# A decoder block on one core: score groups of both kinds in one slot, the router's negated maximum on ScalarE, and later slots for what shares its bank

## The reference

```
x = layernorm(x + mixer(x))            # y = (s + D) * gated, y @ W_out.T + b_out + x
q, k, v = x @ Wq.T + bq, ctx @ Wk.T + bk, ctx @ Wv.T + bv      # 16 heads of 16
x = layernorm(x + softmax(q k^T / 4) v @ Wo.T + bo)
idx, pmax = argmax(softmax(x @ Wr)), max(softmax(x @ Wr))      # 8 experts
pos = running count of idx over all 4096 tokens; kept = pos < 640
out = where(kept, expert_idx(x) * pmax, x)
x = layernorm(x + out)
```

## Time and profile before

| | us |
|---|---|
| median of 3 runs | 1017.29 (1015.42 to 1017.44) |
| profiled execution | 1020.84, its span 1019.1 |
| TensorE busy in the span | 863.1 (85%) |
| VectorE | 597.7 (59%) |
| ScalarE | 405.0 (40%) |
| GpSimd | 354.1 (35%) |
| mean granted TensorE clock | 0.909 |

### The profile page before, as it was taken

The page is one execution under the profiler, slowest core; times in us unless marked ns, Lnnn a source line. Parts: engine busy times, 40 slices in busy tenths (PEclk is TensorE's granted clock), DMA queues, the critical chain, the costliest instruction groups (busy, mean ns, idle before and its releaser), DMA issues. The chain is left out here.

```text
span 1019.1 us, 16854 instructions
## 1 busy us (share of the span) xinstructions
PE 863.1 (85%) x5964; PEld 663.5 (65%) x5964; DVE 597.7 (59%) x1441; ACT 405.0 (40%) x623; POOL 354.1 (35%) x290
## 2 busy tenths in 40 slices
PE   5998947789899888988989888887279999999993
PEld 4776725455666566655666556544279999999993
DVE  4889751545675777667676666643235555555542
ACT  4565611145444444445444454443043334233320
POOL 0333352222233434344342443223212442244422
PEclk9999967679998999999999998877579999999997
DMA  3117302444443445444344442400343222343100
GB/s 115 42 43 210 108 24 78 113 106 126 104 126 115 109 111 125 124 113 114 103 124 121 117 114 74 116 21 24 106 135 109 94 88 90 113 128 106 46 22 22
DMA packets 73432, 98.82 MB, mean 97 GB/s; under 512 B 10529, under 2 KB 60874, under 8 KB 73376
## 3 DMA queue, kind: packets, MB, share of 16 engines
q1 hardware_dynamic: 69920, 89.95, 32.0%
q0 software_dynamic: 3456, 8.13, 2.2%
HBM read 63.40 MB, written 35.73 MB: 97 GB/s over the span
## 5 line engine op out<-in xcount | busy, mean ns | idle before, releaser
L946 DVE TENSOR_REDUCE nmax<-ps_m 128x4 f32<-128x1024 f32 x128 | 156.6, 1224 | 174.6 <-PE ps_m L711 172.1
L903 ACT ACTIVATE pt<-ps_a 128x1024 f32<-128x1024 f32 x128 | 131.1, 1025 | 89.7 <-PE ps_a L721 88.3
L1216 ACT ACTIVATE hid<-ps_h 128x640 fp32r<-128x640 f32 x64 | 45.1, 705 | 151.3 <-PE ps_h L1156 151.3
L1156 PE MATMUL ps_h<-xt,w_hi 128*128 128x320 f32 x512 | 99.9, 318 | 1.0 <-DVE xt L1231 1.0
L1168 PE MATMUL ps_y<-w_hi,hid 128*128 128x256 f32 x640 | 85.3, 284 | 1.7 <-issue 1.7
L1265 DVE SCALAR_TENSOR_TENSOR hid<-ps_h,hid 128x640 fp32r<-128x640 f32 x64 | 52.7, 824 | 56.2 <-ACT hid L1216 55.7
L1156 PEld LDWEIGHTS ps_h<-xt,w_hi 128*128 128x128 f32 x512 | 80.0, 191 | 5.5 <-DVE hid L1265 3.9
L1168 PEld LDWEIGHTS ps_y<-w_hi,hid 128*128 128x128 f32 x640 | 80.1, 192 | 1.9 <-issue 1.9
L721 PE MATMUL ps_a<-qst,kst 49*128 49x256 f32 x512 | 67.8, 345 | 15.5 <-ACT pt L903 15.2
L721 PEld LDWEIGHTS ps_a<-qst,kst 49*128 49x128 f32 x512 | 40.8, 197 | 57.0 <-issue 31.8
L711 PE MATMUL ps_m<-kst,qst 48*128 48x256 f32 x512 | 66.9, 342 | 11.1 <-DVE nmax L946 5.9
(11 more groups left out here) (169 smaller groups left out, 1654.9 us busy)
## 6 DMA issues: line engine op xcount, KB each, us to landing
halves_dram<-half SPq DMA_DIRECT2D x64, 256.0 KB, 2.4
gated<-in_w SPq DMA_DIRECT2D x16, 1024.0 KB, 5.4
kst<-halves_dram SPq DMA_DIRECT2D x64, 128.0 KB, 3.1
qst<-halves_dram SPq DMA_DIRECT2D x64, 128.0 KB, 3.2
rows_dram<-blank SPq DMA_DIRECT2D x1, 5160.0 KB, 19.7
gated<-rows_dram SPq DMA_DIRECT2D x8, 645.0 KB, 4.2
x_raw<-in_x_t SPq DMA_DIRECT2D x8, 512.0 KB, 3.9
xres<-in_x SPq DMA_DIRECT2D x16, 256.0 KB, 3.6
```

The source lines that it names most:

```text
L903: nc.scalar.activation(pt[:, k % 4].rearrange("p s t q -> p (s t q)"), ps_a[:].rearrange("p s t q -> p (s t q)"), ACT.Exp).then_inc(s["exp ...
L946: nc.vector.tensor_reduce(nmax[:, q, :, :, h // 2].rearrange("p t s -> p s t"), ps_m[:], AX.X, ALU.max, negate=True).then_inc(s["max_done" ...
L1156: mm = pe.matmul(ps_h[:, f % 2, c2, 0:HC], w1[a][:, p, k, f * P:(f + 1) * P], xt[:, b, p, k, c2 * HC:(c2 + 1) * HC], start=(n == 0 and k = ...
L1216: nc.scalar.activation(hid[:, HI, f, :].rearrange("p (c n) -> p c n", c=2), ps_h[:, f % 2, :, 0:HC], ACT.Relu).then_inc(s["hid_hi"], 1)
```

## The change

TensorE's step, ScalarE's and VectorE's are reordered, and one operation changes its engine. Nothing of the arithmetic is changed.

- `AL` goes from 3 to 4: `scores_t` of a pair moves one slot later, to the even slots, and is written right behind that slot's `scores`. `weigh` keeps its slot and stands right behind them.
- TensorE: x2's transposes from slot 1 to 2, `router` from 2 to 4, `count` from 6 to 7, `sums_by_query` from 7 and 9 to 8 and 10, `values` from 9 and 10 to 8 and 9, `spread_s` from 12 to 11, the transposes of `onrm` from 11 to 12, both `project_out` together in 14 (were 12 and 13), `mixer_out` in 13 and 15 (were 14 and 15).
- `ntop` is made by ScalarE (slot 6, ahead of the `Exp`), and `el` moves to slot 7.
- VectorE: the statistics, mean and variance of the first norm come ahead of x2; logits, maxima and indices stand in slot 5, behind the reduction of slot 4; place and slot move a slot later; `y` from 13 to 12; the second norm's sum from 14 to 15.

```diff
-    AL, WL = 3, 5
+    AL, WL = 4, 5
@@ TensorE, step; the new order (the old one: slots as listed above)
                 for h in range(NH):
                     if h % 2 == 0 and on(n, 1):
                         scores(n - 1, q, h // 2)
                     j, head, lag = behind(n, h, AL)
                     if head % 2 == 0 and on(n, lag):
                         scores_t(j, p if lag == 2 else q, head // 2)
+                    if h == 0 and on(n, 2):
+                        maxima_rows(n - 2, p)
+                    j, head, lag = behind(n, h, WL)
+                    if head % PV == PV - 1 and on(n, lag):
+                        weigh(j, p if lag == 2 else q, head // PV)
+                    if h == 1 and on(n, 0):
+                        keys(n, p, 0)
+                    if h == 2 and on(n, 4):
...
+                        turn(ps_e, pay[:, p], s["x2t_mm"])
+                    if h == 2 and on(n, 0):
+                        keys(n, p, 1)
+                    if h == 4 and on(n, 4):
+                        router(n - 4)
                     if h == 5 and on(n, 0):
...
                         turn(ps_d, x1, s["x1t_mm"])
+                    if h == 7 and on(n, 4):
+                        count(n - 4)
                     if h == 7 and on(n, 0):
                         queries(n, 0)
                         queries(n, 1)
+                    if h in (8, 10) and on(n, 3):
+                        sums_by_query(n - 3, (h - 8) // 2)
+                    if h in (8, 9) and on(n, 1):
+                        values(n - 1, q, h - 8, n if on(n, 0) else None)
+                    if h == 11 and on(n, -1):
+                        spread_s(n + 1)
+                    if h == 12 and on(n, 3):
                         pe.wait_ge(s["on_done"], 2 * (n - 3) + 2)
                         turn(ps_e, onrm, s["ont_mm"])
+                    if h in (13, 15) and on(n, -1):
+                        mixer_out(n + 1, (h - 13) // 2)
+                    if h == 14 and on(n, 3):
+                        project_out(n - 3, 0)
+                        project_out(n - 3, 1)
@@ ScalarE, step
-                    if h == 5 and on(n, 4):
+                    if h == 6 and on(n, 0):
+                        act.wait_ge(s["x1t_mm"], n + 1)
+                        nc.scalar.copy(x1t[:].rearrange("p k t -> p (k t)"), ps_d[:]).then_inc(s["x1t_out"], 1)
+                    if h == 6 and on(n, 4):
+                        act.wait_ge(s["top_out"], n - 3)
+                        nc.scalar.mul(ntop[:], top[:, :, 0], -1.0).then_inc(s["ntop_out"], 1)
+                    if h == 7 and on(n, 4):
                         j = n - 4
                         act.wait_ge(s["ntop_out"], j + 1)
...
@@ copy of ont: slot 12 to 13; of vals: 11 to 10; of x2t: behind the Exp of slot 2, not ahead
@@ VectorE, step
-                    if h == 0 and on(n, 4):
+                    if h == 0 and on(n, 0):
+                        dve.wait_ge(s["r1_done"], n + 1)
+                        stats(st1, r1, s["stats1"])
+                    if h == 1 and on(n, 0):
+                        mean_var(dc, st1, mv1, s["stats1"], n)
+                        nc.vector.tensor_scalar(ve1[:], mv1[:, :, 1], EPS, None, ALU.add).then_inc(s["var1_ready"], 1)
+                    if h == 1 and on(n, 4):
                         dve.wait_ge(s["rstd2"], i + 1)
...
-                    if h == 3 and on(n, 4):
+                    if h == 5 and on(n, 4):
+                        need(dve, s["ntop_out"], i)
                         dve.wait_ge(s["logit_mm"], i + 1)
...
-                    if h == 4 and on(n, 4):
+                    if h == 5 and on(n, 4):
+                        dve.wait_ge(s["vo_row"], 1)
                         dve.wait_ge(s["top_out"], i + 1)
-                        nc.vector.tensor_scalar(ntop[:], top[:, :, 0], -1.0, None, ALU.mult).then_inc(s["ntop_out"], 1)
...
@@ selection 6 to 7, place 7 to 8, slot 8 to 9, dest 9 to 10; onrm 8, 10 to 9, 11; r2 14 to 15
-                    if h == 13 and on(n, -1):
+                    if h == 12 and on(n, -1):
                         dve.wait_ge(s["sbc_mm"], n + 2)
```

More of the change, by code:

```diff
@@ L784, in step @@
                         scores(n - 1, q, h // 2)
-                    if h == 0 and on(n, 2):
-                        maxima_rows(n - 2, p)
                     j, head, lag = behind(n, h, AL)
@@ L789, in step @@
                         scores_t(j, p if lag == 2 else q, head // 2)
[L790 to L795, removed]
+                    if h == 0 and on(n, 2):
[6 more added lines that the diff above has]
+                    if h == 2 and on(n, 4):
+                        pe.wait_ge(s["x2_done"], n - 3)
+                        if on(n, 2):
+                            pe.wait_ge(s["m_out"], n - 1)
+                        turn(ps_e, pay[:, p], s["x2t_mm"])
[3 more added lines that the diff above has]
+                        router(n - 4)
                     if h == 5 and on(n, 0):
@@ L873, in step @@
                         add_bias(c["b_k"], s["k_out"])
-                    if h == 6 and on(n, 0):
-                        act.wait_ge(s["x1t_mm"], n + 1)
-                        nc.scalar.copy(x1t[:].rearrange("p k t -> p (k t)"), ps_d[:]).then_inc(s["x1t_out"], 1)
                     if h == WL and on(n, 3):
@@ L884, in step @@
                         add_bias(bq, s["q_out"])
-                    if h == 12 and on(n, 3):
+                    if h == 13 and on(n, 3):
                         act.wait_ge(s["ont_mm"], n - 2)
                         nc.scalar.copy(ont[:].rearrange("p k t -> p (k t)"), ps_e[:]).then_inc(s["ont_out"], 1)
-                    if h == 11 and on(n, 1):
+                    if h == 10 and on(n, 1):
                         act.wait_ge(s["v_mm"], n)
@@ L905, in step @@
                                              ).then_inc(s["exp_done"], 1)
+                    if h == 2 and on(n, 4):
+                        act.wait_ge(s["x2t_mm"], n - 3)
+                        nc.scalar.copy(x2t[:].rearrange("p k t -> p (k t)"), ps_e[:]).then_inc(s["x2t_out"], 1)
             run(act, step)
@@ L962, in step @@
                         nc.vector.tensor_copy(pay[:, p, :, D], c["tokens"][:, bass.ds(i * KT, KT)])
[L963 to L968, removed]
                     if h == 2 and on(n, 4):
@@ L1002, in step @@
                         rc.done(nc.vector.tensor_scalar(slot0[:], expert[:], float(CAP), -1.0, ALU.mult, ALU.add))
-                    if h == 6 and on(n, 4):
+                    if h == 7 and on(n, 4):
                         dve.wait_ge(s["cum_mm"], n - 3)
@@ L1007, in step @@
                         nc.vector.tensor_tensor(carry[:], carry[:], hot[:, 0, :], ALU.add).then_inc(s["place_done"], 1)
-                    if h == 7 and on(n, 4):
+                    if h == 8 and on(n, 4):
                         dve.wait_ge(s["sel_out"], n - 3)
@@ L1012, in step @@
                         nc.vector.tensor_tensor(carry[:], carry[:], hot[:, 1, :], ALU.add).then_inc(s["carry_ready"], 1)
-                    if h == 8 and on(n, 4):
+                    if h == 9 and on(n, 4):
                         dve.wait_ge(s["place_out"], n - 3)
@@ L1018, in step @@
                         nc.vector.reciprocal(pay[:, p, :, D + 1], den[:]).then_inc(s["pay_ready"], 1)
-                    if h == 9 and on(n, 4):
+                    if h == 10 and on(n, 4):
                         dve.wait_ge(s["over_out"], n - 3)
                         nc.vector.tensor_tensor(dest[:, p, :], slot[:], over[:], ALU.add).then_inc(s["dest_ready"], 1)
-                    if h in (8, 10) and on(n, 3):
-                        t = (h - 8) // 2
+                    if h in (9, 11) and on(n, 3):
+                        t = (h - 9) // 2
                         dve.wait_ge(s["ot_mm"], 2 * j + t + 1)
@@ L1031, in step @@
                                                 ).then_inc(s["on_done"], 1)
-                    if h == 14 and on(n, 3):
+                    if h == 15 and on(n, 3):
                         dve.wait_ge(s["oproj_mm"], j + 1)
```

3 lines of the change are left out of this document (removed).

## The result

The changed kernel takes 978.03 us (median of 4 runs, 976.36 to 978.56) against 1016.36 (4 runs, 1011.73 to 1017.44): ratio 0.9628, 95% interval 0.9595 to 0.9661, 38 us less.

What follows compares the result with a forecast made beforehand. TensorE was taken to set the pace. A step of 28.2 us plus 0.4 (port) and 0.5 (clock) gave 29.1 against 31.98; 34.6 over twelve steps plus 3 for ramps made 37.6 less, so 980 us, range 963 to 1004.

Steps and rivals of the forecast that it cites:

- Pairing: Score groups side by side on TensorE: 0.31 us saved for each of seven new pairings, 2.0 a step (bounds 1.5 and 3.5).
- TensorE's work: A clean step without its waits: 27.3 us before, 25.3 after; slot by slot the costs came to 25.4.
- Keys: Keys' matmuls wait 0.5 us for VectorE's residual sum, which stands behind a reduction; 0.2 of it was there before.
- x2's transposes: TensorE waits 0.3 us for x2, since VectorE now does the first norm's statistics, mean and variance ahead of it.
- Count: TensorE's wait for the one-hots falls from 1.30 to 0.6 us.
- Mixer: New TensorE wait of 1.3 us for `y`, which VectorE makes only after reductions and the second normalisation.
- The port: GpSimd's power may get between x2's two VectorE operations, making x2 0.7 us later; taken as 0.4 a step.
- The clock: Loss to the lowered clock falls from 1.0 to 0.5 us a step (bounds 0 and 1.7).
- The ramps: Steps 2, 3 and 16, outside the twelve full steps: worth at most 2.0 us each, half taken, 3 together.
- Rival 1: GpSimd's power slips between x2's operations in every step, 0.7 us instead of 0.4: 984 us; chance 0.20.
- Rival 2: The mixer's wait pulls the clock down for the matmuls behind it: 992 us, up to 1012; chance 0.17.
- Rivals 3 to 5: Mixer doesn't wait, 958 (0.10); pairing worth nothing, about 1017 (0.04); slower by the wait for `y`, 1046 (0.06).

Runs made afterwards that it cites:

- the pairing alone: Kernel before with only the second score group of a pair one slot later, right behind the first (AL = 4): 993.13 us, ratio 0.9771.
- `y` first: Changed kernel with the four operations of `y` on VectorE ahead of the maximum reduction of slot 12: 959.42 us, ratio 0.9436 to before.
- reduction between: Changed kernel with indices and one-hots behind the reduction of slot 6 instead of ahead of it: 1005.81 us, ratio 0.9885 to before.

## Why the prediction held, step by step

The forecast of 980 came out at 978, and the two sums beneath it agree as well: 29.1 against 29.09 a step, 34.6 against 34.7 us over the twelve. Part of this is luck, as its terms show, and so is the last step from the sum to the median. The sum forecast 37.6 us between the two profiled executions, and they lie 44.5 apart. The medians lie 38.3 apart because the profiled execution before was 4.5 above its median and that of the changed kernel 1.7 below; I had corrected by 3.55 and taken the changed kernel's to be alike. That hid a sum that was 6.9 too small, all of it in the ramps.

- *Pairing*, 0.31 each, 2.0 in all: the work fell by 2.1 (27.70 to 25.64). The price of one is 0.26, 0.35 or 0.39, as the place has it; between full matmuls the entrance costs as much as my upper bound of 0.2 allowed, behind the weighing nothing. What of the 2.1 is the rest of the reordering I can't say: the pairing alone gave 1.8.
- *TensorE's work*, 25.4: the clean step of 28.45 less its four stalls (0.68, 0.40, 0.66, 1.07: 2.81) leaves 25.6. My way there was off: the waits of the clean step before are 3.28 (0.17, 1.30, 0.95, 0.41, 0.45), not 3.7. There is none for the first normalisation, which I put at 0.6, and 0.41 of the sums by query I had not counted. So the work before was 27.7 and not 27.3.
- *Keys*, 0.5: 0.68 in this step and 0.46 in the next. *x2's transposes*, 0.3: 0.40 and 0.23. *Count*, 0.6: 0.66 and 0.60. *Exponential*, none: none. All four were right in kind and within 0.2.
- *Mixer*, 1.3: 1.07, and right in its cause, as `y` first showed. It is the largest thing that the change gave back: 18.6 us with what hangs on it.
- *The tiny negation on ScalarE*, 0.2 to 0.3: 0.21.
- *The port*, 0.4: nothing. x2's two operations ran unbroken, 0.73 or 0.74 together in every full step. GpSimd's power ran beside them and took 0.70 to 0.84, where it took 0.69 before:

```profile
409.37 0.73 DVE L971 TENSOR_SCALAR pay<-r,mv,ve 128x256 f32<-128x256 f32 x2
...
409.44 0.70 POOL L591 TENSOR_TENSOR ve<-ve,power 128x2 f32<-128x2 f32 x1 [2.46 <-DVE ve L965]
...
439.35 0.84 POOL L591 TENSOR_TENSOR ve<-ve,power 128x2 f32<-128x2 f32 x1 [2.78 <-DVE ve L965]
```

  The Trainium skill's page "SBUF — State Buffer", section "Who interferes with whom", has the lock go to whoever issues first, and the other stand until it is free. This trace does not bear that out for these operations: neither stood for the other's length. In the step from 435.91 the power's row even starts 0.04 ahead of x2's (439.39), and x2 was not late. How the lock works between them stays open.
- *The clock*, 0.5: 0.64 (29.09 less 28.45). The size was close, its working was not. I expected the falls to thin out because the longest stall shrinks, and wrote that none would be left behind the queries; there was one in six of the twelve steps, nearly every second. Each costs its step some 1.6 of work (27.24 instead of 25.6).
- *The ramps*, 3: 9.9 in the profiled execution. This was the worst term. What follows step 15 gave 6.9 of it, step 16 alone (28.52 to 23.78) 4.7. Much of that is the clock in these two executions: the granted clock was 0.52 in 652 to 666, half of step 16 before, and is 0.57 in 621 to 625 and in 607 to 615, of which only the last 5 us are in step 16. No run tells how much of it every execution would give.

Rival 1 is refuted by x2's 0.73 or 0.74 in every full step. Rival 2 (the mixer's wait pulls the clock down behind it) has a true half: the wait does take part in the falls, but the matmuls right behind the mixer run at full speed, 1.92 for eight. Rivals 3 to 5 did not occur. The bound for the loads was rightly put: they wait 5.4 in all, 3.8 of it at the first group of step 16, and as the step gets shorter they rise to 9.7, 10.7 and 12.9.

## What to carry to other kernels

Put groups of matmuls of one tiling next to each other: here each change of tiling there and back cost 0.26 to 0.39 us of a step of 30. In an order written by hand, walk each engine's queue past the new order and ask which operation with someone waiting (here `y`, `r1`, the one-hots) stands behind one for which nobody waits yet, and which work that could run (here the queries) stands behind a waiting instruction. Moving `y`, `r1` and the queries gave 35 us on top of the change's 38. Judge an edit in the order in which it will stand: the negation's move was worth 12 us in the old order and nothing that can be told in the new.

## What the runs showed of the hardware that I had not expected

- The clock's fall behind the count (0.58 in 474 to 478) disappeared in all full steps but the last when either of two stalls was removed, the 0.66 right ahead of it or the 1.07 some 17 us ahead. With only one of them in the step, the granted clock was 1.00 over 329 and 332 us. With a stall of 2.06 at the count (reduction between) there was a fall in each of the twelve steps. With both stalls left and only the keys' wait gone there were two.
- A `tensor_scalar` on 128x2 values took 0.94 us in one place, 0.36 in another (445.30) and 0.16 or 0.17 where it is shortest. In both of the longer cases it ended within 0.03 of GpSimd's subtraction.
